# Interleaving the gates' chain of a gated delta-rule layer with the first group's convolution taps

## What is computed

```
x  = x + layernorm(attention(layernorm(x)))
x  = x + layernorm(moe_ffn(layernorm(x)))

attention(x):
  qkvz = x @ W_qkvz.T            # 16 groups: q, k (128 each), v (2 x 128), z (2 x 128)
  b, a = x @ W_ba.T              # 32 heads each
  q, k, v = silu(causal conv with 4 taps over the tokens (q, k, v))
  beta = sigmoid(b)
  g    = -exp(A_log) * softplus(a + dt_bias)      # the gates
  h = gated delta rule in chunks (q, k, v, cumulative g, beta)
  out = (norm_w * rmsnorm(h) * silu(z)) @ W_out.T
```

## Time and profile before

| | us |
|---|---|
| median of 3 runs (lowest, highest) | 1457.39 (1455.38, 1457.75) |
| the profiled execution's own time | 1462.19 |
| its span, first to last instruction | 1459.8 |
| PE busy in it | 1314.2 (90%) |
| DVE busy | 1078.9 (74%) |
| ACT busy | 975.6 (67%) |
| POOL busy | 665.2 (46%) |
| mean granted TensorE clock | 0.971 of full speed |

### The profile page before, as it was taken

The page is one execution under the profiler, slowest core; times in us unless marked ns, Lnnn a source line. Parts: engine busy times, 40 slices in busy tenths (PEclk is TensorE's granted clock), DMA queues, the critical chain, the costliest instruction groups (busy, mean ns, idle before and its releaser), DMA issues.

```text
span 1459.8 us, 33841 instructions
## 1 busy us (share of the span) xinstructions
PE 1314.2 (90%) x11516; PEld 912.9 (63%) x11516; DVE 1078.9 (74%) x2142; ACT 975.6 (67%) x2122; POOL 665.2 (46%) x726
## 2 busy tenths in 40 slices
PE   2679999999999999999999999999987469999995
PEld 2246676766666666766666666667666336666663
DVE  4577978879797979788797979788765445555555
ACT  2569788887989798888989797988865122222221
POOL 0125554546455454545464455545463306555550
PEclk9999999999999999999999999999999659999998
DMA  2111010101010110101010110100010024455441
GB/s 83 44 37 47 29 37 24 38 23 45 16 45 24 47 43 23 38 23 41 20 45 16 45 45 31 38 23 16 23 41 9 1 71 166 150 151 153 151 153 36
DMA packets 44656, 76.34 MB, mean 52 GB/s; under 512 B 7172, under 2 KB 26022, under 8 KB 44488
## 3 DMA queue, kind: packets, MB, share of 16 engines
q1 hardware_dynamic: 44488, 74.19, 16.3%
HBM read 72.85 MB, written 1.32 MB: 51 GB/s over the span
## 4 chain that ended last, share of the span: by engine, by line
PE 68%; DVE 18%; issue 6%; ACT 6%; DVEq 1%; DMA 0%; SPq 0%; POOL 0%; ACTq 0%; POOLq 0%
PE bank L561 12%; PE bank L779 8%; DVE sil L1132 7%; PE products L732 6%; PE products L709 5%; PE bank L515 4%; PE products L515 4%; PE bank L617 3%; PE products L605 3%; PE products L723 3%; PE bank L637 3%; DVE t L1189 3%; PE bank L645 3%; PE products L712 2%; PE bank L580 2%
## 5 line engine op out<-in xcount | busy, mean ns | idle before, releaser
L561 PE MATMUL bank<-xT,whl 128*128 128x512 f16 x1152 | 305.7, 382 | 13.4 <-DVE sil L1132 9.3
L1378 POOL TENSOR_TENSOR hsq<-hsq,qsq 128x512 f32<-128x512 f32 x64 | 81.4, 1273 | 483.5 <-ACT hsq L982 483.5
L1132 DVE SCALAR_TENSOR_TENSOR sil<-bank,cw,sil 128x510 f32<-128x510 f32 (+2 forms) x384 | 283.2, 737 | 9.7 <-ACT sil L854 4.3
L1189 DVE CAST_PREDICATED t<-levm,bank 128x256 f16<-128x256 uint8 x384 | 165.5, 431 | 114.1 <-PE bank L637 57.0
L1021 ACT ACTIVATE kq<-vtok 128x512 f16<-128x512 f32 x94 | 59.2, 630 | 192.1 <-DVE vtok L1309 192.1
L950 ACT ACTIVATE x<-bank 128x256 f16<-128x256 f32 x320 | 123.5, 386 | 94.6 <-PE bank L617 89.9
L1202 DVE CAST_PREDICATED u<-levm,bank 128x256 f16<-128x256 uint8 x384 | 162.9, 424 | 0.0
L561 PEld LDWEIGHTS bank<-xT,whl 128*128 128x128 f16 x1152 | 93.9, 98 | 85.6 <-DVE sil L1132 13.7
L779 PE MATMUL bank<-wmhl,kq 128*128 128x256 f16 x1128 | 138.4, 273 | 0.3
L617 PE MATMUL bank<-t,n 128*128 128x64 f16 x1536 | 109.6, 194 | 25.9 <-DVE t L1189 23.1
L617 PEld LDWEIGHTS bank<-t,n 128*128 128x128 f16 x1536 | 80.3, 98 | 83.6 <-DVE t L1189 61.7
(11 more groups left out here) (159 smaller groups left out, 3153.6 us busy)
## 6 DMA issues: line engine op xcount, KB each, us to landing
grow<-rowsc SPq DMA_DIRECT2D x64, 256.0 KB, 3.3
wt<-wqkvz SPq DMA_DIRECT2D x16, 768.0 KB, 4.5
wms<-wm SPq DMA_DIRECT2D x47, 256.0 KB, 4.1
zs<-gsc SPq DMA_DIRECT2D x18, 512.0 KB, 3.9
wo<-wout SPq DMA_DIRECT2D x16, 256.0 KB, 3.8
zs<-gsc SPq DMA_DIRECT2D x8, 448.0 KB, 3.8
zs<-gsc SPq DMA_DIRECT2D x8, 384.0 KB, 3.6
zs<-gsc SPq DMA_DIRECT2D x9, 320.0 KB, 3.6
```

What stands on the lines that cost most here:

```text
L561: mm = nc.tensor.matmul(dst[:, :], whl[:, h, k, col:col + HD], xT[:, l, k, half * 512:(half + 1) * 512], start=(k == 0 and m == 0), stop=( ...
L1132: nc.vector.scalar_tensor_tensor(out=dst[:, :, late:S], in0=src[:, :, 0:S - late], scalar=cw[:, q, i, 3 - late:4 - late], in1=dst[:, :, la ...
L1189: nc.vector.copy_predicated(halves(t16[:, pair(U)], n)[:, :, :, 0], by4(2 * n, n), packed(X_BANK, n)).then_inc(s_tup, 1)
```

## The change

- **Tokens' load.** `xs` counts on a semaphore of its own, `s_xin`; `s_const` now has seven loads (112). DVE starts the statistics on `s_xin`, and waits for `s_const` after them. ACT waits for `s_const` only ahead of the copies of the transposed tokens. The level masks' copy (L1056) moves on DVE behind the low halves of the tokens.
- **Loads' order.** `xs`, `cst`, `wba`, then group 0's `wt` and `cw`, then `eye`, `lev`, `dtb`, `alog`, `normw`.
- **Weights early.** Group 0's `hi` (ACT) stands directly behind the reciprocal deviations, and its `lo` (DVE) directly behind the normalization, ahead of the low halves of the tokens. `sequence()` no longer yields them.
- **The gates' chain in four pieces.** `sequence()` yields `gate` 0 to 3 for group 0 behind taps 2, 5, 8 and 11. DVE's four pieces hold the steps up to GD_ABS, up to GD_G, the reciprocal (GD_BETA), and the rest. ACT has pieces 0, 1 and 3; PE has one piece (k = 2) with the three cumulative products; SP has one piece (k = 3), the rows' store and loads, which now stands behind the load of group 1's weights. PE's waits for the finished gates move into the first `kk`, DVE's into the first `sc`.

```diff
@@ sequence()
-    yield "rows", 0, (None, 0)
...
-                    if (-1 if part in ("hi", "lo", "weights") else 0) <= g < HQK:
+                    if (-1 if part == "weights" else 0) <= g < HQK:
                         yield part, i, (None, g)
+                    if g == 0 and part == "tap" and i % 3 == 2 and i // 3 < GATES:
+                        yield "gate", i // 3, (None, 0)
@@ block.sync
-            sp.dma_start(xs[:], x.rearrange("(t p) d -> p t d", p=P)).then_inc(s_const, 16)
+            sp.dma_start(xs[:], x.rearrange("(t p) d -> p t d", p=P)).then_inc(s_xin, 16)
             sp.dma_start(cst[:], c32).then_inc(s_const, 16)
+            sp.dma_start(wba_sb[:], wba.rearrange("(k p) n -> p k n", p=P)).then_inc(s_const, 16)
+            sp.dma_start(wt[:], wqkvz[:, :, 0]).then_inc(s_w, 16)
+            sp.dma_start(cw[:, 0], convw[:, 0]).then_inc(s_w, 16)
             sp.dma_start(eye[:], eye16).then_inc(s_const, 16)
             sp.dma_start(sq[:, 0:6 * P], lev.rearrange("p k i -> p (k i)")).then_inc(s_const, 16)
-            sp.dma_start(wba_sb[:], wba.rearrange("(k p) n -> p k n", p=P)).then_inc(s_const, 16)
...
-            load_group((None, 0))
@@ block.tensor
+            def gate(F, k):
+                if k < 2 or k > 2:
+                    return
+                pe.wait_ge(s_gd, GD_G)
+                nc.tensor.matmul(bank[3][:, 0:256], upper, scal[:, C_G].rearrange("p h t -> p (h t)"), start=True, stop=True).then_inc(s_ba, 1)
...
             def kk(U, _):
                 (G, b), q = U, U[0][1] % 2
+                if unit_index(U) == 0:
+                    pe.wait_ge(s_gd, GD_SCAL)
+                    pe.wait_ge(s_gcol, 1)
+                    pe.wait_ge(s_growc, 1)
@@ block.scalar
+            def gate(F, k):
+                if k == 0:
+                    act.wait_ge(s_ba, 1)
...
+                elif k == 1:
+                    act.wait_ge(s_gd, GD_ABS)
...
+                elif k == 3:
+                    act.wait_ge(s_grow, 1)
...
+            for k in range(2):
+                high_weights((None, -1), k)
+            act.wait_ge(s_const, 112)
+            copy_transposed(0)
@@ block.vector
+            dve.wait_ge(s_xin, 16)
             statistics(xs, GD_ST1)
+            dve.wait_ge(s_const, 112)
             split_small(wba_sb[:], 0, 2 * HV)
             normalize(xn, xs, 2)
...
+            def gate(F, k):
+                if k == 0:
+                    dve.wait_ge(s_ba, 1)
+                    dve.wait_ge(s_ga, 1)
...
+                elif k == 1:
+                    settle()
+                    step(nc.vector.tensor_scalar(zb[:], zb[:], 0.0, None, ALU.max))
+                    settle()
+                    dve.wait_ge(s_ga, 4)
...
+                elif k == 2:
+                    step(nc.vector.tensor_scalar(za[:], za[:], 1.0, None, ALU.add))
+                    settle()
+                    step(nc.vector.reciprocal(scal[:, C_BETA], za[:].rearrange("p t h -> p h t")))
...
+                elif k == 3:
+                    settle()
+                    dve.wait_ge(s_ga, 6)
...
+            for k in range(2):
+                low_weights((None, -1), k)
+            low_transposed(0)
+            nc.vector.tensor_copy(levm[:].rearrange("p k i -> p (k i)"),
+                                  sq[:, 0:6 * P]).then_inc(s_levm, 1)
```

More of the change, by code:

```diff
@@ L17 @@
 BEHIND = 2
+GATES = 4
 TOK = B * S
@@ L441, in load_row @@
                              .partition_broadcast(P)).then_inc(s_row[n % 2], 16)
-            def rows(F, _):
+            def gate(F, k):
+                if k < GATES - 1:
+                    return
                 sp.wait_ge(s_growc, 1)
@@ L458, in next_weights @@
                     load_group((None, F[1] + 2))
-            load_group((None, 0))
-            attention({"rows": rows, "row": next_row, "weights": next_weights, "owts": load_out_weights})
+            attention({"gate": gate, "row": next_row, "weights": next_weights, "owts": load_out_weights})
             sp.dma_start(b1s[:], b1).then_inc(s_mconst, 16)
@@ L539, in _ @@
             mm.then_inc(s_ba, 1)
[L541 to L553, removed]
+            def gate(F, k):
+                if k < 2 or k > 2:
+                    return
+                pe.wait_ge(s_gd, GD_G)
+                nc.tensor.matmul(bank[3][:, 0:256], upper, scal[:, C_G].rearrange("p h t -> p (h t)"), start=True, stop=True).then_inc(s_ba, 1)
+                nc.tensor.matmul(bank[4][:, 0:256], below, scal[:, C_G].rearrange("p h t -> p (h t)"), start=True, stop=True).then_inc(s_ba, 1)
+                for n in range(2):
+                    mm = nc.tensor.matmul(bank[5][:, n * P:(n + 1) * P],
+                                          scal[:, C_G].rearrange("p h t -> p (h t)")[:, n * P:(n + 1) * P], upper,
+                                          start=True, stop=True)
+                mm.then_inc(s_grow, 1)
             def projected(F, n, k):
@@ L734, in proj @@
                 mm.then_inc(s_op, 1)
-            attention({"fill": fill, "rest": rest, "kk": kk, "x": x, "w": w, "y0": y0_, "y1": y1_, "y2": y2_, "p": p,
+            attention({"gate": gate, "fill": fill, "rest": rest, "kk": kk, "x": x, "w": w, "y0": y0_, "y1": y1_, "y2": y2_, "p": p,
                        "o": o, "ss": ss, "proj": proj})
@@ L818, in _ @@
             rsqrt_var(GD_ST1, 1)
[L819 to L835, removed]
@@ L995, in inverse_root @@
                 nc.scalar.activation(hrs[:, pair(U)], hrs[:, pair(U)], ACT.Exp, scale=-0.5).then_inc(s_rr, 1)
-            attention({"evict": evict, "hi": high_weights, "silu": silu, "nexp": norm, "cap": cap, "exb": row_factors,
+            for k in range(2):
+                high_weights((None, -1), k)
+            act.wait_ge(s_const, 112)
+            copy_transposed(0)
+            attention({"gate": gate, "evict": evict, "hi": high_weights, "silu": silu, "nexp": norm, "cap": cap, "exb": row_factors,
                        "exp": factors, "cross": cross_, "n16": high_n, "xe": xe, "g": guess, "vn": solved,
@@ L1093, in _ @@
-            assert done[0] == GD_ABS
-            settle()
-            step(nc.vector.tensor_scalar(zb[:], zb[:], 0.0, None, ALU.max))
-            settle()
-            dve.wait_ge(s_ga, 4)
-            step(nc.vector.tensor_tensor(zb[:], zb[:], zc[:], ALU.add))
-            settle()
-            rate = alog_sb[:].unsqueeze(2).to_broadcast([P, HV, NT])
-            step(nc.vector.scalar_tensor_tensor(out=scal[:, C_G], in0=zb[:].rearrange("p t h -> p h t"), scalar=-1.0,
-                                                in1=rate, op0=ALU.mult, op1=ALU.mult))
@@ L1103, in _ @@
-            assert done[0] == GD_G
-            step(nc.vector.tensor_scalar(za[:], za[:], 1.0, None, ALU.add))
-            settle()
-            step(nc.vector.reciprocal(scal[:, C_BETA], za[:].rearrange("p t h -> p h t")))
-            assert done[0] == GD_BETA
-            settle()
-            dve.wait_ge(s_ga, 6)
-            flat = lambda a: a.rearrange("p t h -> p (t h)")
-            step(nc.vector.tensor_scalar(flat(scal[:, C_NEG]), flat(za[:]), -1.0, None, ALU.mult))
-            step(nc.vector.tensor_tensor(flat(scal[:, C_ELB]), flat(zb[:]), flat(scal[:, C_BETA]), ALU.mult))
@@ L1147, in scalars @@
                 q, f = F[1] % 2, group_index(F)
+                if F[1] == 0:
+                    dve.wait_ge(s_gd, GD_SCAL)
+                    dve.wait_ge(s_gcol, 1)
                 wait_g(dve, s_v0s, before(F, 2), 8, 8)
```

72 lines of the change are left out of this document (44 added, 28 removed).

## The result

The changed kernel takes 1449.99 us (median of 16 runs, 1447.05 to 1454.76), the kernel before 1457.61 (16 runs, 1455.38 to 1463.73). The ratio is 0.9943, 95% interval 0.9932 to 0.9955: 7.6 us less. The forecast was 8.8 less (1448.6) and a range of 1445.0 to 1452.5.

The account below looks back on a forecast made before the run. It took a serial chain through DVE, ACT and PE to bound the head, and DVE the taps. Head 2.5, taps 7.1, less 0.8 for stalls, gave 8.8 us off the median 1457.39: 1448.6, range 1445.0 to 1452.5.

Parts of the forecast that it names:

- Head: Ahead of the gates' product: statistics start on the tokens at 6.3, constants complete at 12.3, everything 2.5 us earlier.
- T: The end of the gates' product, at 27.13 before; forecast to move by 2.5 us to 24.6.
- First tap: After the gates' product only the first fill and rest and one evict remain: tap 0 at T + 2.22, gain 11.56.
- I take the pair at full clock: Fill 0 and rest 0 on PE, ahead of tap 0: no idle stretch before them, so 1.47 us.
- Pieces: DVE's gates' steps between the taps: 5.22 added less 0.77 saved behind taps, net 4.45 us; 5.6 without overlap.
- rival 1: Between the taps: the gates' pieces cost in full, no overlap, 1.15 us more, so 1449.8; chance 0.10.
- Waits: New waits among taps and pieces if PE runs at 0.50: 0.8 us taken, from 0 to 3.
- rival 2: In the pieces: PE's idle gaps bring clock 0.50 and stalls of 3.0 instead of 0.8, so 1450.8; chance 0.14.
- Behind the last tap: From sc through the first kk: same work, only the clock can differ, up to 2.7 us either way; taken as 0.
- rival 3: The stretch behind the last tap wins as well, no stall and part of the 2.7 us: 1445.9; chance 0.08.
- Sum: Whole kernel: 2.5 + 7.1 - 0.8 = 8.8 us less, from the median 1457.39 to 1448.6.
- 13.78 us: Everything between 27.13 and 40.91, removed from in front of tap 0.

Follow-up runs that it names:

- e3: The changed kernel, but DVE waits for all constants ahead of the statistics; 1454.64 us, ratio 0.9962 to the kernel before.
- e4: The changed kernel with the loads in the order of before, the tokens' semaphore kept; 1450.97 us, ratio 0.9944 to the kernel before.
- e7: e4 plus two idle matmuls on PE in each empty fill or rest slot while the last units run; 1448.82 us, ratio 0.9929 to the kernel before.
- e9: e4 with each of the gates' four pieces one place earlier, piece 0 ahead of tap 0; ratio 0.9956 to the kernel before.
- e8: The kernel before with only 17 idle matmuls, between group 0's transposes of v and ahead of the first kk; ratio 1.0003 to the kernel before.
- e1: The changed kernel with the head's edits alone, the gates' chain ahead of all slots again; 1453.65 us, ratio 0.9963 to the kernel before.
- e2: Interleaving of the gates alone, with loads' order, statistics behind all constants and weights' slots as before; 1452.41 us, ratio 0.9943 to the kernel before.
- e11: e4 with group 0's weights split in their slots ahead of fill 0, gates still interleaved; ratio 0.9951 to the kernel before.
- e10: e4 with idle matmuls on PE wherever runs had shown half clock, from head to drain; 1443.81 us, ratio 0.9903 to the kernel before.
- e5: The changed kernel with idle matmuls in the head, between group 0's transposes of v and ahead of the first kk; 1450.66 us, ratio 0.9938.

## Why the prediction was right, point by point

- **Head.** Forecast: constants complete at 12.3, all 2.5 us earlier. Measured 12.00, and 2.8 (T 24.30 against 27.13). `normw` took 5.8, as read in the earlier trace rows; `xs` took 6.1 and not 5.6, so the statistics began at 6.87 and not 6.3, which the 1.75 us of DVE's wait ahead of 12.00 covered. `lo` was covered, as worked out, by 0.23. e3 shows the wait that this removed, e4 that the loads' new order is no part of the gain but takes 1.1 of it; the prediction had the 1.4 in its sum, and did not set it apart as a loss that could be had back.
- **First tap.** Forecast T + 2.22, measured T + 2.80. The step that failed is "I take the pair at full clock": the first weight loads of fill 0 stand 0.42 apart up to 25.37, as they did in the kernel before under a granted clock of 0.50 (38.67, 39.10, 39.52), and behind it 0.21. I had taken the head's shown 1.00 at its word. Size: 0.6.
- **Pieces.** Forecast 4.45 net for four. From the first tap to `sc` it is 24.59, against 20.27 before (61.18 - 40.91): 4.32. A piece's first step starts 0.66 behind the tap ahead of it (28.81 to 29.47, the third tap of three at 0.85), so rival 1, with 5.6, falls: an independent step starts before the one ahead has ended. The prediction had given only half of what the Trainium skill says (VectorE: DVE Perf Modes, The DRAIN you can't avoid): the same paragraph adds that a next op which is not held starts earlier, and with that the trace agrees.
- **Waits.** None showed in the profile; 0.8 was taken. e7 shows one of 1.0 in an execution in which the clock among the taps fell, and e9, with the pieces in other places, 2.0. So rival 2's mechanism exists, but it is rare: of the nine profiles with the pieces where the change has them, eight take 24.6 from the first tap to `sc` and only e7 25.5, a mean of 0.1. The 0.8 was too much.
- **Behind the last tap.** Taken as 0, with 2.7 either way. The profile shows 2.2 gained up to t, as rival 3 had it, and 2.6 more in the drain, which the prediction had not named at all. e8 and e3 show for the first that it is the clock. The drain's is shown only in part: over eleven profiles the time goes with the granted clock there, but where matmuls were added to raise it, it moved by less (e7: 0.5 us against e4).
- **Sum.** 2.8 + 7.1 - 0.6 + 0.1 = 9.5 at the last tap (9.49 measured), against a forecast 9.6 less 0.8. The medians moved by 7.6 and not by 9.5; the runs of each kernel spread over 8 us with their clock (the prediction had reckoned with 2.9), and the interval of the ratio is 6.6 to 9.9 us. Runs at the same mean clock, 0.979, differ by 8.9, which speaks for the 9.5 in every execution and for the mix of clocks as what the medians lack; what brings that mix stays open. That the forecast of the median is only 1.2 off is partly luck: the 0.8 for waits that did not come made up for some of it.
- **The parts overlap.** The sum had the weights' split in the 13.78 us removed between T and the first tap, rightly. But it would have been wrong to credit either part alone: e1 and e2 together give 15.1 us of shift, the whole gives 9.5, and e11 at most 0.4 for the early split.

## What to carry to other kernels

A chain of small steps with waits between engines costs little when it is dealt out between the steps of another chain that waits for itself: here 5.5 us of DVE work cost 4.3, and removed 11 us of waiting. Cost such parts together, not one by one, for two edits may remove the same wait; and look for the edit in a bundle that takes something back. Where TensorE works with pauses, compare kernels by the best and the spread of many runs, not by two profiles: two executions of one kernel differ by 8 us here, as much as the change is worth, and filling the pauses with matmuls that nobody reads gave 0.4% more (e10 against e4).

## What the runs showed of the hardware that was not expected

- The granted clock is shown as 1.00 from the start of the span, while the work runs at half rate: eight transposes take 1.94 us in the head, 1.06 behind idle matmuls (e5); the gates' product 2.74, the same as under a shown 0.50 in e5, and 1.57 in e10. Read the head's clock from the spacing of like matmuls. The Trainium skill (TensorE: Matmul & The Clock Gate, What's actually happening) has it that the throttled state is the default and activity releases it; the runs agree, the shown value does not.
- Little decides whether the rate holds: in e5 it fell behind pauses of 1.44 and 1.27 us, with eight short transposes between them; in e10, with pauses of 0.49 and 1.27, it held.
- Idle matmuls cost nothing where they stand ahead of a wait that is long anyway (e10: 17.39 from `sc` to t), and 0.4 us behind such a wait (e5, e8: 17.8 and 17.9).
